# One product for gate and up of the last hidden chunk, earlier layer-1 queries, and a last output tile summed row by row, in a gated cross-attention kernel

## The reference, cut to what matters

```python
x = x + tanh(g_xattn[0]) * L0_xattn(layernorm(x), ctx, ctx)     # 32 query heads, 8 key heads
x = x + tanh(g_ffn[0])   * L0_ffn(layernorm(x), ...)            # hidden width 704, weights as integers
x = x + tanh(g_xattn[1]) * L1_xattn(layernorm(x), ctx, ctx)     # 16 query heads, 4 key heads, then @ Wc.T + bc
x = x + tanh(g_ffn[1])   * L1_ffn(layernorm(x), ...)            # 32 experts of width 96, top 8 by the router
# L0_ffn
W = (wq - 128) * scale[:, None]
out = (silu(x @ Wg.T) * (x @ Wu.T)) @ Wd.T
# L1_ffn: masked_w is the softmax of the 8 highest router logits of a token, zero elsewhere
h = silu(g) * u * masked_w[:, :, None]
out = einsum('tei,ehi->th', h, w_down_proj)
```

## Time and profile before

| | us |
|---|---|
| runs | 422.61, 425.23, 424.72 |
| median of the runs | 424.72 |
| profiled execution, its own time | 426.17 |
| profiled execution, its span from first to last instruction | 424.3 |
| busy in it: PE, DVE, ACT, POOL | 387.4, 302.2, 220.7, 174.2 |

### The profile page before, as it was taken

How to read it: one execution, slowest core, us unless ns; L and a number is a source line. 1 busy time by engine, 2 the same in 40 slices (tenths; PEclk the granted TensorE clock), 3 DMA queues, 4 the chain that set the end, 5 groups by cost and what they waited for, 6 DMA issues and landing times.

```text
span 424.3 us, 6897 instructions
## 1 busy us (share of the span) xinstructions
PE 387.4 (91%) x2258; PEld 336.1 (79%) x2258; DVE 302.2 (71%) x612; ACT 220.7 (52%) x441; POOL 174.2 (41%) x201
## 2 busy tenths in 40 slices
PE   4888989989977987969999999999999999999994
PEld 3777879979967977958788778888787888888883
DVE  5699888777755777677777676665877666666664
ACT  3577866556455653545655544445444444444431
POOL 5954332512435113247534343554353444353510
PEclk9999899989998999999999999999999999999999
DMA  5911211110000110032221211223223243323101
GB/s 132 274 45 49 50 28 31 50 44 0 2 0 10 21 20 3 4 110 76 75 76 54 72 50 63 76 74 108 70 85 100 86 133 104 103 84 111 39 0 49
DMA packets 20818, 27.16 MB, mean 64 GB/s; under 512 B 10928, under 2 KB 13616, under 8 KB 20784
## 3 DMA queue, kind: packets, MB, share of 16 engines
q1 hardware_dynamic: 20784, 26.73, 21.7%
HBM read 24.36 MB, written 1.05 MB: 60 GB/s over the span
## 4 chain that ended last, share of the span: by engine, by line
PE 48%; DVE 4%; ACT 1%; SPq 1%; issue 1%; DMA 1%; POOL 0%; DVEq 0%; ACTq 0%
PE bank L1298 14%; PE bank L1300 14%; PE bank L1299 14%; PE bank L1195 1%; SPq L461 1%; PE bank L1218 1%; PE bank L1176 1%; PE bank L1156 1%; PE bank L1385 1%; DMA kbd<-khl 1%; DVE t_t L1012 0%; DVE h_t L1018 0%; DVE t_t L999 0%; DVE hl L1023 0%; POOL wl L558 0%
## 5 line engine op out<-in xcount | busy, mean ns | idle before, releaser
L558 POOL TENSOR_TENSOR wl<-wraw,wh 128x768 fp32r<-128x768 f32 x48 | 88.8, 1850 | 105.1 <-DVE hl L1023 105.1
L1298 PE MATMUL bank<-xh,wh 128*128 128x512 f32 (+1 forms) x288 | 108.5, 377 | 2.8 <-DVE t_t L999 2.7
L1300 PE MATMUL bank<-xh,wl 128*128 128x512 f32 (+1 forms) x288 | 102.5, 356 | 0.0
L1299 PE MATMUL bank<-xl,wh 128*128 128x512 f32 (+1 forms) x288 | 102.3, 355 | 0.0
L656 ACT ACTIVATE hh<-h_t 128x512 fp32r<-128x512 f32 (+1 forms) x72 | 40.3, 560 | 98.7 <-DVE h_t L1018 81.2
L1298 PEld LDWEIGHTS bank<-xh,wh 128*128 128x128 f32 x288 | 54.9, 191 | 10.7 <-DVE t_t L999 2.2
L1023 DVE TENSOR_TENSOR hl<-h_t,hh 128x512 fp32r<-128x512 f32 (+1 forms) x72 | 43.4, 603 | 24.8 <-ACT hh L656 24.7
L1300 PEld LDWEIGHTS bank<-xh,wl 128*128 128x128 f32 x288 | 54.6, 190 | 7.9
L1299 PEld LDWEIGHTS bank<-xl,wh 128*128 128x128 f32 x288 | 55.0, 191 | 6.7
L999 DVE SCALAR_TENSOR_TENSOR t_t<-s_t,bank 128x512 f32<-128x512 f32 (+1 forms) x72 | 42.9, 595 | 23.6 <-ACT s_t L791 23.0
L1298 PE MATMUL bank<-hh,wh 128*128 128x512 f32 (+1 forms) x144 | 51.6, 359 | 8.7 <-DVE x L1034 5.3
(11 more groups left out here) (106 smaller groups left out, 571.9 us busy)
## 6 DMA issues: line engine op xcount, KB each, us to landing
wraw<-w SPq DMA_DIRECT2D x54, 384.0 KB, 3.1
kbd<-khl SPq DMA_DIRECT2D x80, 8.0 KB
out<-x SPq DMA_DIRECT2D x8, 128.0 KB, 2.5
kbd<-khl SPq DMA_DIRECT2D x40, 16.0 KB
x<-x_in SPq DMA_DIRECT2D x2, 256.0 KB, 3.7
ctx_v<-ctx_in SPq DMA_DIRECT2D x2, 256.0 KB, 6.2
x<-x_in SPq DMA_DIRECT2D x1, 512.0 KB, 5.6
ot<-sel_in SPq DMA_DIRECT2D x1, 512.0 KB, 5.2
```

Source lines behind the costliest of these rows:

```text
L558: ops.tensor_tensor(wl[:, slot, :], wraw[:, i % WRAW, :], wh[:, slot, :].bitcast(F32), ALU.subtract).then_inc(F.w_split, 1)
L1298: nc.tensor.matmul(o, wh[:, slot, w_sl], rh, start=first, stop=False, skip_group_check=reopened)
L1299: nc.tensor.matmul(o, wh[:, slot, w_sl], rl, start=False, stop=False, skip_group_check=reopened)
L1300: return nc.tensor.matmul(o, wl[:, slot, w_sl], rh, start=False, stop=stop, skip_group_check=reopened)
```

## The change

1. **The half-empty chunk.** In steps 5, 11, 17 and 23 the 64 gate rows stand in partitions 0 to 63 and the 64 up rows in 64 to 127 of one set of weights. `gate(s)` does nothing there; one product of six, in the place of `up(s)`, gives both into the up bank. tanh and L999 read that bank, and the multiplication takes its upper half against the lower.
2. **One copy** of a unit's transposed weights (128 x 512) in place of two halves, and one wait in `values`.
3. **Layer-0 weights.** ACT first makes a float copy `wf` (`w_float`, new) and rounds it to wh; wl is a subtraction on POOL, at its tick 4, 7, 10, 13, 16 and 19, in place of DVE. A raw buffer is loaded again after `wf`.
4. **Experts.** `weigh` stands ahead of the multiplication by up, and `spread` ahead of `up(s)` in place of within `down(s - 1)`; m_done comes with the finished product.
5. **Start of layer-1 attention.** `q_split` of tile 1, its layer norm, `q_copy` and PE's `q_transposes` of tile 0 move from one step ahead of `START` to two steps ahead, `q_split` of tile 1 with it in front of `power` of tiles 2 and 3.
6. **The end.** The output of the second pass of experts is taken out after chunk 69 (of 0 to 71), put back into PSUM transposed by `open_rows` (full float32 products with the identity, so that the bank stays open), and the last two chunks add to it in rows of tokens (`down_rows`: 12 products of 256 columns a chunk). DVE adds two tiles at once (`add_pair`).

```diff
+def halved(s):
+    return s < MOE0 and s % F0 == F0 - 1
...
             def load(i):
                 if i >= WRAW:
-                    sp.wait_ge(F.w_split, i - WRAW + 1)
+                    sp.wait_ge(F.wf_ready if i - WRAW < F0 else F.w_split, i - WRAW + 1)
...
+                if n >= 4 and (n - 4) % 3 == 0 and (n - 4) // 3 < F0:
+                    w_low((n - 4) // 3)
...
-                for j in (0, 2):
-                    copy(pts[:, n % 2, j:j + 2, :], bank[a.p_bank(n)][:, j * P:(j + 2) * P].rearrange(
-                        "p (j c) -> p j c", c=P)).then_inc(a.pts_ready, 1)
+                copy(pts[:, n % 2], bank[a.p_bank(n)][:].rearrange("p (j c) -> p j c", c=P)).then_inc(a.pts_ready, 1)
...
+            def w_float(i):
+                act.wait_ge(F.w_loaded[i % WRAW], 16 * (i // WRAW + 1))
+                if i >= 2:
+                    act.wait_ge(F.w_split, i - 1)
+                nc.scalar.activation(wf[:, i % 2, :], wrawi[:, i % WRAW, :], ACT.Copy, bias=-ZERO_POINT
+                                     ).then_inc(F.wf_ready, 1)
...
                 if i < F0:
-                    nc.scalar.activation(wh[:, i, :], wrawi[:, i % WRAW, :], ACT.Copy, bias=-ZERO_POINT
-                                         ).then_inc(F.wh_ready, 1)
+                    act.wait_ge(F.wf_ready, i + 1)
+                    copy(wh[:, i, :], wf[:, i % 2, :]).then_inc(F.wh_ready, 1)
...
-            def w_low(i):
-
-                dve.wait_ge(F.wh_ready, i + 1)
-                ops.scalar_tensor_tensor(wl[:, i, :], wrawi[:, i % WRAW, :], -ZERO_POINT, wh[:, i, :].bitcast(F32),
-                                         ALU.add, ALU.subtract).then_inc(F.w_split, 1)
...
-                if s + 1 in START:
-                    layer_norm(A[1], START[s + 1] * HT + 1)
-                    q_copy(A[1], START[s + 1] * HT)
-            take_out(2 + QP - 1)
+                if s + 2 in START:
+                    layer_norm(A[1], START[s + 2] * HT + 1)
+                    q_copy(A[1], START[s + 2] * HT)
...
+                if halved(s):
+                    ops.scalar_tensor_tensor(h_t[0:HALF, k, 0:w], bank[UB][HALF:P, 0:w], suh[0:HALF, c:c + 1],
+                                             t_t[0:HALF, k, 0:w], ALU.mult, ALU.mult).then_inc(F.m_done, 1)
...
+            def add_pair(i):
+                t0 = tiles(QP + 1)[2 * i]
+                dve.wait_ge(F.pair_done, i + 1)
+                ops.scalar_tensor_tensor(x[:, t0:t0 + 2, :], bank[BACK[1][2 * i]][:].rearrange("p (t d) -> p t d", d=DM),
+                                         tg[:, 3:4], x[:, t0:t0 + 2, :], ALU.mult, ALU.add).then_inc(F.x_done, 2)
...
             def gate(s):
+                if halved(s):
+                    return
...
             def up(s):
...
+                if halved(s):
+                    if s < F0:
+                        pe.wait_ge(F.w_split, s + 1)
+                    projection(s, UB, 0).then_inc(F.g_done, 1)
+                else:
+                    projection(s, UB, DM).then_inc(F.u_done, 1)
...
+            def open_rows():
+                pe.wait_ge(F.ot_act, KC * QP + 2)
+                pe.wait_ge(F.ot_dve, 2)
+                pe.wait_ge(F.x_done, TT + HT)
+                for t in range(HT):
+                    for h in range(KC):
+                        nc.tensor.matmul(bank[BACK[1][t]][:, t % 2 * DM + h * P:t % 2 * DM + (h + 1) * P],
+                                         ot[:, h, t * P:(t + 1) * P], ident[:], start=(t % 2 == 0 and h == 0), stop=False,
+                                         skip_group_check=True)
+            def down_row(s, t, hs, ws):
+                return nc.tensor.matmul(bank[BACK[1][t]][:, t % 2 * DM:(t % 2 + 1) * DM], hs[:, s % 2, t * P:(t + 1) * P],
+                                        ws[:, slot_of(s), 2 * DM:3 * DM], start=False, stop=last(s), skip_group_check=True)
+            def down_rows(s):
+                pe.wait_ge(F.hh_ready, s + 1)
+                for t in range(HT):
+                    down_row(s, t, hh, wh)
+                    down_row(s, t, hh, wl)
+                pe.wait_ge(F.h_split, s + 1)
+                for t in range(HT):
+                    done = down_row(s, t, hl, wh)
+                    if last(s) and t % 2:
+                        done.then_inc(F.pair_done, 1)
...
+                if s == STEPS - 1:
+                    open_rows()
                 for k, n in beside(s, 0):
                     tick(k, n)
+                if s > MOE0 and (s - MOE0) % CPQ == 0:
+                    spread(s)
                 up(s)
+                if s == MOE0:
+                    spread(s)
                 if s:
-                    down(s - 1)
+                    down_rows(s - 1) if by_rows(s - 1) else down(s - 1)
...
-                if s + 1 in START:
-                    q_transposes(A[1], START[s + 1] * HT)
-            down(STEPS - 1)
-            for t in range(HT):
-                back_tile(QP + 1, t)
+                if s + 2 in START:
+                    q_transposes(A[1], START[s + 2] * HT)
+            down_rows(STEPS - 1)
```

More of the change, by code:

```diff
@@ L35 @@
 MC = EXPERTS * INNER // P
+HALF = HIDDEN - (F0 - 1) * P
 NEG = -3.0e38
@@ L137, in backs, with ups, gate_bank, by_rows @@
     return p * QT if p < QP else TT + (p - QP) * HT
+def halved(s):
+    return s < MOE0 and s % F0 == F0 - 1
+def ups(s):
+    return sum(not halved(i) for i in range(s + 1))
+def gate_bank(s):
+    return UB if halved(s) else GB
 def width(s):
     return QTOK if s < MOE0 else BLK
+def by_rows(s):
+    return s >= STEPS - ROWS
 def quad(s):
@@ L646, in _ @@
                     q_split(A[1], t)
+                if s + 2 in START:
+                    q_split(A[1], START[s + 2] * HT + 1)
                 if s + 1 in START:
@@ L649, in _ @@
                     power(A[1], t + 2, t + 4)
-                    q_split(A[1], t + 1)
         @block.scalar
@@ L749, in tick0 @@
                     exp(a, n)
+                if 2 <= n < 2 + 3 * F0 and (n - 2) % 3 == 0:
+                    w_float((n - 2) // 3)
                 if 3 <= n < 3 + 3 * F0 and (n - 3) % 3 == 0:
@@ L814, in take_out @@
                 else:
-                    copy(ot[:, 0, :], bank[DB[p][0]][:], tg[:, 3:4]).then_inc(F.ot_act, 1)
+                    copy(ot[:, 0, :], bank[DB[p][0]][:], tg[:, 3:4] if p == QP else 1.0).then_inc(F.ot_act, 1)
             def route_exp(h):
@@ L969, in tick0 @@
                     shift(a, n, done)
-                if n >= 4 and (n - 4) % 3 == 0 and (n - 4) // 3 < F0:
-                    w_low((n - 4) // 3)
                 if n == 26:
@@ L1115, in _ @@
             split_h(STEPS - 1)
-            take_out(QP + 1)
-            for t in range(HT):
-                add_tile(QP + 1, t)
+            for i in range(HT // 2):
+                add_pair(i)
         @block.tensor
@@ L1327, in up @@
                     pe.wait_ge(F.m_done, s)
-                tok = tokens(pass_of(s))
-                for h in range(KC):
-                    done = product(bank[UB][:, 0:width(s)], slice(DM + h * P, DM + (h + 1) * P), slot_of(s),
-                                   xh[:, h, tok], xl[:, h, tok], h == 0, h == KC - 1)
-                done.then_inc(F.u_done, 1)
+                if halved(s):
+                    if s < F0:
+                        pe.wait_ge(F.w_split, s + 1)
+                    projection(s, UB, 0).then_inc(F.g_done, 1)
+                else:
+                    projection(s, UB, DM).then_inc(F.u_done, 1)
             def down(s):
@@ L1347, in down @@
                     done = product(bank[DB[p][h]][:, at:at + w], slice(2 * DM + h * P, 2 * DM + (h + 1) * P),
-                                   slot_of(s), hh[:, k, 0:w], hl[:, k, 0:w], first(s) and (h == 0 or p >= QP), last(s),
-                                   reopened=True)
-                    if h == 0 and s + 1 >= MOE0 and s + 1 < STEPS and quad(s + 1) * CPQ == s + 1 - PASS[pass_of(s + 1)][0]:
-                        spread(s + 1)
+                                   slot_of(s), hh[:, k, 0:w], hl[:, k, 0:w], first(s) and (h == 0 or p >= QP), last(s) or s + 1 == STEPS - ROWS, reopened=True)
                 done.then_inc(F.dn_done, 1)
```

98 lines of the change are left out of this document (56 added, 42 removed).

## The result

The changed kernel takes **419.17 us** (median of 9 runs, 416.74 to 422.89), the kernel before 424.72 beside it (422.61 to 425.23): ratio 0.9885, 95% interval 0.9847 to 0.9923. A second comparison on another occasion gave 418.59 against 424.95: 0.9841 (0.9791 to 0.9891). All executions pooled, the medians are 419.02 (15) and 424.69 (64), a gain of 5.7 us where 7.8 was forecast. The profiled execution took 419.08 us, span 416.9, against 426.17 and 424.3.

A forecast was written before the change was run, and what follows sets the result against it. No engine throughout: DVE in the attention alone, waits at the start of layer-1 attention, PE in the second expert pass; gains 1.5 + 1.2 + 1.3 + 3.3 + 0.5 = 7.8 us from 424.72 gave 416.9, range 413.0 to 421.5.

The forecast's parts named there:

- START: Start of layer-1 attention: query split and transposes one step earlier remove step 14's 2.89 us wait; gain 3.3 (2.0 to 4.1).
- the half-empty chunk: Steps 5, 11, 17, 23: one group of six products fewer each; gains 0.5, 0.3, 0.5 and 0, together 1.3 us.
- Attention alone and steps 0 to 3: Layer-0 weight subtractions leave DVE, keys load earlier: gain 1.5 us (0 to 2.3), then 1.2 (0 to 2.1).
- the first rival: Attention alone: ACT takes DVE's place as the bound, first two terms give 0 instead of 2.7; 419.6 us, chance 0.20.
- The end: Row-wise sums of the last two chunks: opening products cost 1.7 us, shorter tail; gain 0.5 (loss 1.1 to gain 1.3).
- the experts' order: Expert steps: weighing before the multiplication by up gains nothing, since PE is full there.
- The second rival: Step 14's wait moves to the exponential and later units' shifts, clock falls, 1.0 of 3.3 stays; 419.2 us, chance 0.13.
- The third and the fourth rival: POOL's subtractions hold DVE in steps 0 to 3: 420.6 us, 0.06; or stand in DVE's unit chain: 429.4, 0.04.

The follow-up runs named there:

- D undone: Changed kernel with layer 1's first query tiles (transposes and copy of tile 0, norm and split of tile 1) one step later again: 420.96 us, ratio 0.9920.

## Why the prediction was right, and where not

The time lay in the range and the sign was right. The sum was 2 us too high, nearly all of it in two terms, START (1.3 too high) and the half-empty chunk (0.6). By its steps:

- **Attention alone and steps 0 to 3 (forecast 1.5 + 1.2):** right in size. Taking the low parts from POOL and giving them back to VectorE costs 1.9 us at step 0 and 3.1 at step 4; undoing all of it 2.8. The reason was half wrong: I had the key transfers and the single copy share in it, and both give nothing by the traces. (The upper bound of 2.3 for the keys is 2.2 by its own numbers, 24.61 + 0.33 - 22.72.) ScalarE at 89% is not yet the bound, so the first rival falls.
- **The half-empty chunk (1.3):** 0.7. Steps 5 and 11 gave 0.4 and 0.25 (forecast 0.5 and 0.3); step 17 gave nothing where I had 0.5, and 0.1 was lost again in step 12, whose wait is 1.54 us with two products and 1.67 with one. The waits for the gate that I put at 0.4 were 0.51 in step 6 and 0.98 in step 12.
- **START (3.3):** 2.0. This is the step that failed. I had seen the new wait for the query split (1.6 forecast, 1.66 measured), and wrote that it lay inside a wait that TensorE had anyway. That holds: where the clock stays up, step 12 costs 6.7 to 6.9 us with the change and 6.81 without. But the term counted the half-clock stretch behind step 14's wait as gained and put none behind the new wait, and in the profiled executions of the changed kernel the stretch moved there. The part gained from up(13) to up(15) was 3.7 us, with the clock in it, where I had 3.25; the clock's price at step 12, which I set to nothing, was 1.7. The 2.0 that is left is the lower bound that I gave, "the clock falls all the same".
- **The end (0.5) and the experts' order (0):** 0.5 and 0.3. For the end the pieces came as forecast too: hl 1.3 us later (8.5 to 9.8 us behind up(70)), and 2.2 us less behind it. Undone in the changed kernel the order costs 1.1, but 0.8 of that exists only with the new end.
- **The second rival** comes nearest by its number (419.2), and in kind: TensorE stood elsewhere, and the clock fell there. The place was step 12, not the exponential's chain that it named. That its number fits to 0.1 us is luck: it left 1.0 of START's 3.3 where 2.0 stayed, and other terms made up for it.
- **The third and the fourth rival** (POOL holding VectorE, POOL in the chain of the units) have little: VectorE's 256-column hl took 0.50 us on average against 0.435, and twice over 1 us, 1.32 at 127.80 us beside POOL's work on the keys (`kbd`), and 1.02 beside one of the moved subtractions:

```profile
63.86 1.83 POOL L584 TENSOR_TENSOR wl<-wf,wh 128x768 fp32r<-128x768 f32 x1
64.96 1.02 DVE L1054 TENSOR_TENSOR hl<-h_t,hh 128x256 fp32r<-128x256 f32 x1
```

hl ends at 65.98, 0.29 us behind POOL's end at 65.69, where alone it takes some 0.43. The Trainium skill, SBUF — State Buffer, section "Who interferes with whom", has the later of two such instructions stand for the whole of the first; this row agrees nearly. It bit little here: of the six moved subtractions none took longer than 1.84 us, and in the attention alone VectorE's row maximum and its subtraction read `bank`, which is PSUM.

The parts add up to 2.8 + 0.7 + 2.0 + 0.5 + 0.3 = 6.3, against 5.7 in the pooled medians, and 5.5 between executions at a clock of 0.996 (416.8 against some 422.3). The 7.4 between the two profiled spans is more than either, and some 0.9 us of it is probably the chance of the first units: the kernel with D undone, which is the changed kernel up to there and has its third unit's subtraction at 17.86 us like the kernel before (17.99), stands 0.9 later at step 0 than the changed kernel's second execution (16.46). What parts 6.3 from 5.7 wasn't found; the intervals allow both.

## What to carry to other kernels

A wait on TensorE costs more than its length where the clock falls behind it: here 1.66 us of waiting were 3.5 us of time in the executions whose clock fell, and 1.9 in those whose clock did not. A half-clock stretch that one wait brings isn't gained by removing that wait if a new one of like length stands just ahead. When a step is moved ahead to save a wait, ask what its new place waits for, and move that input too; the change gained 3.7 us in steps 13 and 14, paid 1.7 at step 12 and left 3.5 to be had there. Moving 6.3 us of work off an engine that is 92% full paid 2.8, while ScalarE, which got conversions for it, rose to 89%; joining two half copies into one, or splitting it again, changed no distance in the traces.

## What was not expected of the hardware

- Stretches of 3.4 us at half clock cost 0.7 us (the one at 176) to 1.7 us each (the one at step 12). From step 7 on they began between 0.5 us ahead of and 1.8 us behind the end of a wait of 1.5 to 2.9 us on TensorE, yet not at each such wait: after the same wait of 1.9 us in step 7 one execution of the same instructions fell to half clock and another did not (windows above), and of the ten traces with the wait of 1.5 to 1.7 us for the query split in step 12, seven fell behind it and three did not. By my estimate from this, a median of six executions carries about a microsecond of chance.
- Full float32 products of 128 columns cost 0.128 us a record, against 0.215 at 256 columns.
- Identical programs stood up to 2.1 us apart at step 0 (49.48 and 51.57), by the first units alone.
